# An attention stage with routing: four normalisations stand earlier on GpSimd, one group is ranked sooner on the vector engine

## What is computed

```python
h = layernorm(x, ln1_w, ln1_b)
x1 = x + out_proj(attention(h))           # 16 heads of 16
xn = layernorm(x1, ln2_w, ln2_b)
probs = softmax(xn @ router_w.T)          # 8 experts
gates, experts = top_k(probs, 2)
...
x = layernorm(x + x1 + sum of the two chosen experts' outputs, weighed by the gates)
```

## Time and profile before

| | us |
|---|---|
| median of three runs | 2649.92 |
| lowest and highest run | 2646.74, 2656.01 |
| the profiled execution | 2645.75 |
| its span, first to last instruction | 2643.8 |
| TensorE busy | 2145.4 (81%) |
| vector engine busy | 1463.9 (55%) |
| scalar engine busy | 933.9 (35%) |
| GpSimd busy | 766.7 (29%) |

### The profile page before, as it was taken

How to read it: one execution, slowest core, us unless ns; L and a number is a source line. 1 busy time by engine, 2 the same in 40 slices (tenths; PEclk the granted TensorE clock), 3 DMA queues, 4 the chain that set the end, 5 groups by cost and what they waited for, 6 DMA issues and landing times. The chain is left out here.

```text
span 2643.8 us, 37351 instructions
## 1 busy us (share of the span) xinstructions
PE 2145.4 (81%) x14118; PEld 1491.5 (56%) x14143; DVE 1463.9 (55%) x2966; ACT 933.9 (35%) x1539; POOL 766.7 (29%) x549
## 2 busy tenths in 40 slices
PE   7978857896498686499668877797999999687898
PEld 5765544564497575499345663485343434235787
DVE  4784773446432567311562454133799999993533
ACT  3423322331011234133323321111676667452543
POOL 1121231213200210100321011203489798973000
PEclk9999978998699687699789988898999999998899
DMA  4217010000697110698200002275201111001000
GB/s 161 73 41 248 17 34 32 1 2 33 236 358 297 58 33 8 233 358 320 66 1 25 1 2 89 80 213 154 88 25 40 31 34 40 25 1 52 1 17 16
DMA packets 104577, 234.22 MB, mean 89 GB/s; under 512 B 10000, under 2 KB 77456, under 8 KB 95440
## 3 DMA queue, kind: packets, MB, share of 16 engines
q1 hardware_dynamic: 95664, 209.81, 22.8%
q0 software_dynamic: 7680, 20.98, 2.4%
q10 hardware_dynamic: 1056, 1.05, 0.1%
HBM read 175.83 MB, written 55.97 MB: 88 GB/s over the span
## 5 line engine op out<-in xcount | busy, mean ns | idle before, releaser
L3631 POOL TENSOR_TENSOR l_attn_ring<-l_attn_ring,l_attn_c_rows 128x1024 f32<-128x1024 f32 x128 | 302.0, 2359 | 85.6 <-DVE l_attn_ring L3520 85.6
L3520 DVE TENSOR_TENSOR_SCAN l_attn_ring<-bank,l_attn_ring 128x512 f32<-128x512 f32 x256 | 299.2, 1210 | 22.6 <-ACT bank L3403 18.1
L164 PE MATMUL bank<-x_features,weights 128*128 128x512 f32 x544 | 260.5, 624 | 27.5 <-ACT x_features L3367 11.2
L3247 PE MATMUL bank<-l_attn_ring,identity 128*128 128x512 f32 x512 | 252.8, 617 | 36.8 <-POOL l_attn_ring L3631 29.8
L3403 ACT ACTIVATE bank<-l_attn_step,l_attn_minus_exp_a_log 128x508 f32<-128x508 f32 x256 | 173.5, 685 | 162.0 <-DVE l_attn_ring L3520 161.6
L164 PEld LDWEIGHTS bank<-x_features,weights 128*128 128x128 f32 x544 | 106.0, 199 | 155.5 <-issue 129.7
L3247 PEld LDWEIGHTS bank<-l_attn_ring,identity 128*128 128x128 f32 x512 | 96.6, 196 | 152.7 <-issue 105.2
L458 DVE TENSOR_REDUCE negmax_slots<-bank 128x16 f32<-128x2048 f32 x48 | 109.8, 2287 | 104.5 <-PE bank L350 104.2
L3514 DVE TENSOR_TENSOR l_attn_ring<-l_attn_step_times_input,bank 128x1024 f32<-128x1024 f32 x128 | 153.4, 1199 | 3.6 <-PE bank L3233 1.8
L3899 PE MATMUL bank<-l_ffn_hidden_high,l_ffn_sign_weights 128*128 128x512 f32 x256 | 99.7, 390 | 0.5 <-ACT l_ffn_hidden_high L3960 0.5
L3899 PE MATMUL bank<-l_ffn_hidden_low,l_ffn_sign_weights 128*128 128x512 f32 x256 | 99.6, 389 | 0.0
(11 more groups left out here) (678 smaller groups left out, 4486.4 us busy)
## 6 DMA issues: line engine op xcount, KB each, us to landing
l_attn_tile_weights<-l_ffn_experts SPq DMA_DIRECT2D x22, 2180.0 KB, 10.1
ffn_experts_tile_weights<-l_ffn_experts_experts SPq DMA_DIRECT2D x37, 1024.0 KB, 8.2
expert_slots<-zeros SPq DMA_DIRECT2D x8, 2048.0 KB, 13.6
l_attn_c_rows<-state_outputs SPq DMA_DIRECT2D x64, 256.0 KB, 3.2
l_ffn_tile_weights<-l_ffn_experts SPq DMA_DIRECT2D x23, 512.0 KB, 4.3
expert_slots<-residual_sum SPq DMA_DIRECT2D x62, 128.0 KB, 8.5
expert_slots<-zeros SPq DMA_DIRECT2D x1, 5888.0 KB, 27.8
l_ffn_tile_x<-expert_slots SPq DMA_DIRECT2D x23, 256.0 KB, 4.1
```

The source lines that it names most:

```text
L164: mm = pe.matmul(out, w[:, f, m * P:(m + 1) * P], src[:, f, :], start=start and f == 0, stop=stop and f == k - 1)
L3247: mm = pe.matmul(net.banks[SUMS[j]][:], net.ident[:], ring[n % 4][:, j, :], start=s == 0, stop=s == STATES - 1)
L3520: nc.vector.tensor_tensor_scan(ring[n % 4][:, j, :], net.banks[DECAY[j]][:], ring[n % 4][:, j, :], 0.0, ALU.mult, ALU.add).then_inc(state_ ...
L3631: tt(ring[n % 4][:], ring[n % 4][:], c_row[:, n % STATES, :].unsqueeze(1).broadcast_to([P, 2, T]), ALU.mult).then_inc(out_ready, 1)
```

## The change

```diff
-ROUTED_STEPS = NB * (GROUPS + 1) + 4
+ROUTED_STEPS = NB * (GROUPS + 1) + 5
...
-ROUTE = {"logits": (9, 13, 17, 20), "shift": (10, 14, 18, 21), "choose": (11, 15, 20, 22), "mark": (12, 16, 20, 22), "place": (13, 17, 21, 23),
-         "weigh": (15, 19, 23, 23)}
+ROUTE = {"logits": (9, 13, 17, 21), "shift": (10, 14, 18, 22), "choose": (11, 15, 19, 23), "mark": (12, 16, 20, 23), "place": (13, 17, 21, 24),
+         "weigh": (15, 24, 24, 24)}
...
                     if b == 0 and g + 2 < GROUPS:
                         first_norm(g + 2)
+                    for of in routed_in(k, "shift"):
+                        shift(of)
                     if b == 2 and 1 <= g <= GROUPS:
...
-                    for kind, do in (("place", place), ("shift", shift), ("choose", choose), ("mark", mark),
+                    for kind, do in (("place", place), ("choose", choose), ("mark", mark),
                                      ("weigh", lambda of: route.weights_dve(chain, of_group(of)))):
...
                 with_bias(0)
                 with_bias(1)
+                for n in range(2 * NB, 3 * NB):
+                    before.normalise(nc.gpsimd, pool.wait_ge, n, normed[:, n, :], net.x_all[:, n, :], h_ready)
+                with_bias(2)
+                for n in range(last, SEQUENCES):
+                    before.normalise(nc.gpsimd, pool.wait_ge, n, normed[:, n, :], net.x_all[:, n, :], h_ready)
                 for g in range(2, GROUPS):
-                    for n in range(NB * g, NB * (g + 1)):
-                        before.normalise(nc.gpsimd, pool.wait_ge, n, normed[:, n, :], net.x_all[:, n, :], h_ready)
-                    with_bias(g)
                     base(g - 2)
                     pool.wait_ge(base_ready, g - 1)
                     for n in range(NB * (g - 2), NB * (g - 1)):
                         after.normalise(nc.gpsimd, pool.wait_ge, n, normed[:, n, :], normed[:, n, :], x_ready)
+                    if g == 2:
+                        with_bias(GROUPS - 1)
                 route.scatter_pool(pool, normed, of_group(0))
```

## The result

The changed kernel took 2636.02 us (median of six runs, 2631.82 to 2640.71), the kernel before 2651.81 us in the runs beside it: ratio 0.9941, 95% interval 0.9924 to 0.9959.

The account below looks back on a forecast made before the run. The prediction took hand-written engine order to bound one stage: TensorE's wait in step 7 and group 2's late slot numbers. 8.59 + 4.05 = 12.64 us off 2649.92 gave 2637.3 us, range 2628 to 2647.

Parts of the forecast that it names:

- Part 1: Step 7: GpSimd normalising group 3 early removes TensorE's 6.38 us wait and slower transposes; 8.59 us, from comparison with step 3.
- port rule: GpSimd's early normalisations: vector engine and GpSimd share a pair of ports, and one can block the other for an instruction.
- Part 2: Stage's end: ranking group 2 sooner ends its scatters 4.05 us earlier; 4.47 if shift(2), charged 0.42, delays nothing.
- The tail: Stage's end: 16 scatters without a gap, group 3's slots ready at 668.8 before 671.5, vector engine 2 us ahead of GpSimd.
- the next stage begins 5.51 us after GpSimd's end: Stage's end: GpSimd's last scatter decides when the next stage starts, 5.51 us later.
- The sum: Whole stage: 8.59 + 4.05 = 12.64 us gained, bounds 10.3 and 13.1.
- The stall goes too: Step 14: the scalar engine's 8.71 us remote wait is missed as well, giving 2628.6 us; chance 0.08.
- The wait only changes its name: Before group 0's scatters: the 8.59 us return as another wait, leaving 4.05 and 2645.9 us; chance 0.14.
- A scatter holds up an engine: Ranking of group 2 or 3: a scatter-time hold of up to 25.7 us lands there, giving 2663.0 us; chance 0.06.

Follow-up runs that it names:

- e1: Kernel before with only GpSimd's new order (group 3's four first normalisations early, with_bias(3) later); ratio 0.9965 to the kernel before.
- e2: Kernel before with only the vector engine's new routing (table, shift ahead of the norm, gate weights last); ratio 0.9984 to the kernel before.
- e7: Changed kernel with group 0's eight scatters issued last of all, behind group 3's; ratio 0.9973 to the kernel before.
- e8: Changed kernel with four of group 0's eight scatters at their old place, four straight ahead of group 1's; ratio 0.9963 to the kernel before.
- e9: Changed kernel with all eight scatters of group 0 straight ahead of group 1's; ratio 0.9975 to the kernel before.
- e5: Changed kernel with weigh(1) back in step 19; one run, next stage 236.92 us after the stage's first context products (changed kernel 232.08).
- e6: Changed kernel with weigh(0) at the end too; one run, next stage 235.20 us after the stage's first context products (changed kernel 232.08).
- e4: Changed kernel with group 0's eight scatters moved behind the second norm of group 2; ratio 0.9964 to the kernel before.

## Why the prediction was right, point by point

**Part 1, 8.59 us: right in size and in place.** Step 7 lost exactly 8.59 us, the wait and the slower transposes behind it, as the comparison with step 3 said. Steps 8 to 12 have the lengths of before to within 0.01 us, so nothing took the wait's place. In e1 the 8.62 us were still there when group 2's slots were ready.

The prediction holds a port rule of the Trainium skill (SBUF — State Buffer, Who interferes with whom) against the new place. The rule does not speak against it: the same section of the Trainium skill says that on Trainium2 a tensor_reduce never contends. The trace agrees: the four normalisations ran beside the vector engine's reduction at 498.08 and took 4.82 us, as they did alone (4.83).

**Part 2, 4.05 us: right, and in both of its terms.** From the copy of group 3's logits to the slots, 4.56 us were gained (6.68 to 2.12 us, in e2 and in the changed kernel alike), where 4.47 were reckoned. shift(2) ahead of the norm was charged with 0.42 us and cost 0.51. On the vector engine, from the copy of group 2's keys (L1225) to the statistics of group 3's second norm (L265), first before, then after:

```profile
645.91 0.18 DVE L1225 COPY l_ffn_attention_prob<-bank 128x32 f32<-128x32 f32 x1
646.03 1.40 DVE L265 BATCH_NORM_STATS2 l_ffn_attention_x_stats<-normed 128x6 f32<-128x256 f32 x4
```

```profile
641.58 0.18 DVE L1225 COPY l_ffn_attention_prob<-bank 128x32 f32<-128x32 f32 x1
...
642.21 1.40 DVE L265 BATCH_NORM_STATS2 l_ffn_attention_x_stats<-normed 128x6 f32<-128x256 f32 x4
```

That is 0.12 us in the two profiles without Part 2 and 0.62 or 0.63 in the nine with it. From the copy of group 2's logits to that of group 3's it is 17.57 us before and 17.56 in e1, and 18.08 in e2 and in the changed kernel. 4.56 less 0.51 is 4.05. The 4.46 us of e2 at the next stage are more because, against 0.10 us lost behind the slots, 0.52 were gained ahead of that stretch: 0.21 at the last products and 0.31 from there to the copy of group 2's logits, where Part 2 has not touched group 2 yet. That e2 comes out at the upper bound of the term, 4.47, is therefore luck.

**The tail.** Scatters without a gap, weights hidden, group 3 ready in time (664.73 against its turn at 668.78): all as said. The prediction has group 3's turn at 675.50 in the kernel before; that row is group 2's eighth scatter, and the ninth stands at 677.03. So the time in hand was 1.5 us more than it reckoned, and its sum is untouched. The one step of the reasoning that does not hold in general is "the next stage begins 5.51 us after GpSimd's end". That distance was 5.5 to 6.4 us in eight of the eleven profiles, 3.74 in e7, 9.13 and 9.68 in e8 and e9. Two ends compete: GpSimd's, with 3.7 us or more behind it, and the vector engine's, with 1.2 us behind it. In the changed kernel the vector engine's cover is therefore, by an estimate from these, not the 1.8 us between the two ends but some 6.7 (684.68 - 1.2 - 676.81).

What lies behind GpSimd's end can be read from the DMA queues, to 0.2 us. The last packet of the queue that the scatters use (q0) moves 1.2 us behind that end in e7 and e8, and 2.8 to 3.8 us behind it in the other nine, in which the loads of the experts' weights (q1) run beside it, in the changed kernel from 673.4 to 681.2. The next stage begins 2.5 to 2.7 us behind that packet in the nine profiles in which GpSimd's end decides. So what it follows is the arrival of the scattered rows and not their last issue, and beside the loads they arrived later.

**The sum.** 13.23 and 13.29 us in the two profiles, 12.64 forecast, 13.1 the upper bound. Behind the 8.59 us of step 7 the stage goes on like this. Step 14 took 17.07 us instead of 18.37, 1.30 less. Step 15 took 9.45 instead of 8.06, and from the last products to the copy of group 2's logits it was 6.71 instead of 8.07; these two are one thing, a stretch of some two us at the lower clock (0.50), which lies in step 15 in the changed kernel (626 to 628 us) and behind the last products in the kernel before (634 to 636), where the eight transposes took 1.97 us instead of 1.09. Then shift(2) lost 0.51, the ranking gained 4.56, and 0.67 were lost behind the slots: 0.14 in the row of 16 scatters and 0.53 between GpSimd's end and the next stage. So the two parts made the 12.64 of the forecast, and what passed it is the 1.30 of step 14 less those 0.67. The 1.30 were not forecast. Step 14, with the remote wait in it, took 17.07 and 17.09 us in the two profiles with both parts and 18.06 to 19.18 in before, e1, e2, e5 and e6. What decides its length stays open, so the 0.6 us beyond the forecast are not shown to belong to the edit.

**The rivals.** *The stall goes too* fell: the wait stayed, 6.46 us instead of 8.71, since the scatters arrive in the same formation; e7 and e9 show that moving the scatters removes it. *The wait only changes its name* fell with step 7. *A scatter holds up an engine* did not happen to this change, but the mechanism exists, and the changed kernel ends just ahead of it: in e8 and e9, in which an unbroken row of scatters begins long before the table, the vector engine took 10.4 and 16.3 us longer from group 3's slots to its last weight. That is under the 25.7 that the rival was priced at, and the 6.7 us of cover take their part of it; the next stage came 1.2 and 6.9 us later than in the changed kernel.

## What to carry to other kernels

A wait made by program order alone is worth the difference to a twin of the step that does not have it; that takes in the slower clock behind the wait, which the idle time leaves out (here 8.59 us against 6.38). Where a queue of indirect scatters ends a stage, what counts is when the first late group gets its numbers, and work that only has to be done by the end belongs behind that, as long as the vector engine's end stays covered. When such an edit is read from single profiles, anchor the comparison inside the stage: here stages behind the same code began up to 6 us apart.

## What the runs showed of the hardware

Engines were held up while indirect scatters ran, in two forms. In step 14 (step 16 in e4) scalar and vector engine waited for 5.4 to 8.8 us although the matmul that they needed stands in the record as long done (in the changed kernel the context products of step 14 are over at 605.13, the copy starts at 610.44; the ends of matmuls in the record are modelled, so it stays open which engine was late). The vector engine went on at the end of the row of eight scatters or up to 1.6 us later, the scalar engine between 2.9 us ahead of that end and 0.1 behind it. Not every row does this: under group 1's eight scatters (644.88 to 655.00 in the changed kernel) no engine has a remote wait.

The second form is that of the table above: from 18.4 to 19.8 us behind the first scatter of an unbroken row on, the vector engine waited 0.3 to 1.2 us for itself, again and again, in e8 and e9 beside rows of 36 and 41 us and in e6 beside 16 scatters. In the changed kernel that was one wait of 0.45 us.

The Trainium skill (Runtime: NRT & Kernel Launch, Instruction fetch mechanics) has instructions fetched through DMA queues. The list of DMA queues names them; for 655 to 684 us of e8, where the vector engine had its gaps, it has one packet in such a queue:

```profile
q0 software_dynamic: 803, 2.18, 20.9%
q1 hardware_dynamic: 271, 2.03, 19.7%
q14 instruction: 1, 0.01, 0.1%
```

One packet can't be some twenty gaps, so those are not fetches. Nor are they the loads of the experts' weights (q1), whose first packet in e8 moves at 678.2, behind all of the gaps but the last. In step 14 of the changed kernel one packet of each of two such queues lies within about a microsecond of the first scatter (602.56), and both are through by 603.8, ahead of the scalar engine's wait, which begins at 603.99; the next one moves behind 619 us. e7 and e9 have the same two packets at the same place of the program and no remote wait there. So the waits of step 14 are not these fetches either. What holds the engines up stays open; that the first form comes and goes with the scatters is shown by e4, e7 and e9, and that the second depends on how long a row has run is read from five profiles and was not tried by itself.
